# Delta's softplus summed in DRAM by accumulating DMAs, and three W1 products moved up between W2 tiles

## The chip, the cores and the metric

One core of a Trainium2 chip runs the whole program. The metric is the device time of one execution in microseconds (us). The engines are named as the profile names them: PE (TensorE), ACT (ScalarE), DVE (VectorE), POOL (GpSimd) and SP (SyncE, which here only issues DMAs). DMAs issued by SP go through the queue q1, those issued by POOL through q0.

## The reference

x is (4, 2048, 512) in fp32. Two stages follow each other, each with a residual; scale, shift and gate of both come from a conditioning vector c.

```
h = layernorm(x) * (1 + ca) + sa
val, gate = split(h @ W_in);  val = silu(conv3(val))
B, C = val @ W_B, val @ W_C                      # 16 states
Delta = softplus((val @ W_delta + delta_base) @ W_tau)
h_t = exp(Delta*A) * h_(t-1) + expm1(Delta*A)/(Delta*A + 1e-6) * Delta * B_t * val_t   # over 2048 tokens
y_t = sum over the 16 states of h_t * C_t
x = x + ga * ((y * silu(gate)) @ W_out + h)
h = layernorm(x) * (1 + cb) + sb
x = x + gb * (top-2 of 8 experts, gated, plus one shared expert: gelu(h @ W1 + b1) @ W2 + b2)
```

The change touches how Delta's softplus is put together, and the order of some W1 products.

## The kernel before

**Tiling.** The 8192 tokens are cut into 16 quarters (`q`) of 512. The scan works on a unit of 128 channels by 1024 tokens; a unit has 16 states, one **slot** each, so there are 512 slots in a row. A **window** H holds 32 slots, r = 0 to 31. In window H the engines do the scan of slots 32H to 32H+31, and between its steps the attention products of quarter `qa` = H+2 and the expert products of quarter `qf` = H-2; `qn` = H+3 is the quarter that is loaded next. Windows run from -3 to 18; those with both a scan and a quarter `qa` are 0 to 13, and two more quarters are made before the scan begins.

**What sets the order.** Nothing is scheduled by a tool. Each engine runs through the same windows and slots; the functions `sync_slot`, `act_window`, `pe_slot` (by the table in `pe_jobs`), `dve_slot` and `pool_slot` say what each adds in a slot r. An engine's work is in program order, and semaphores hold the engines together.

**A slot's scan work.** ACT makes `inv` (square, Ln, Exp), `th` (Tanh) and `abar` (Exp) in groups of four states, up to some slots ahead. POOL multiplies `inv` by `th` (line 1316, for two slots ahead), multiplies the state by the row of C (line 1295, for the slot before) and issues a DMA that adds the product into `ysum` in SBUF (line 1303); only one of these is in flight, since each waits for the one before. DVE does four passes over PSUM and SBUF (lines 1099, 1106, 1086, 1092) and the scan itself (line 1119). The scan of slot c writes a buffer of three, so it waits until the addition of slot c-3 has landed. PE puts the row of B for the next slot into PSUM (line 1065) as the first thing of its slot; the other products of the slot are queued behind it. At the end of a unit (r = 1 and 17) POOL waits for the last addition and multiplies `ysum` by the gate (line 1309).

**Delta before.** The product with W_tau (kind `p`, slots 9 and 10 on PE) is taken from PSUM by ACT (`take_p`, line 739) into `pre`. ACT makes exp(-|pre|) in `lnw` and, in place, relu(`pre`); DVE rounds `tt1` = (1+e)-1 (`rounded`, line 1147); POOL makes `tt1 - lnw` (`correction`, line 1340); ACT makes Ln(1+e) in `lnw`; POOL subtracts `tt1` (`log1p`, line 1346, slots 16 and 19); DVE adds min(relu, 1e18) and `lnw` (`softplus`, line 1154, at the end of slots 16 and 20); SP stores the half (slots 17 and 21). All this is done in two halves of two channel groups, 128x1024 each. The buffers are borrowed: `pre` is `hT`, `lnw` is `xa` and `tt1` is `uu`. So `xa`'s next contents, the tokens of `qn` (slots 19 and 21 on SP, line 617), can only be loaded when the half is done with, and DVE takes their statistics (`tile_stats`, line 1124) at the end of slots 21 and 22.

**Expert products.** Line 1038 is a W1 product (one hidden half of one expert: 4 matmuls, 8 instructions in the trace), line 1054 a W2 tile (6 matmuls, 12 instructions). Four PSUM banks are passed round the products of all kinds in the order of the table; a product waits until the one before it in its bank has been taken. W1 weights have two buffers.

## Time and profile before

| | us |
|---|---|
| median of 3 runs | 5096.31 (5090.79 to 5102.79) |
| the profiled execution | 5096.16 |
| its span | 5094.4 |
| DVE busy | 4214.9 (83%) |
| ACT busy | 4024.4 (79%) |
| PE busy | 3923.5 (77%) |
| POOL busy | 3723.2 (73%) |

The span is the time from the first instruction to the last; 1.8 us lie around it. Busy times are of the whole span, and the scan runs in only part of it: its first instruction starts at 276.9 us, its last at 4707.1 us. Before it the first two quarters are made, behind it the last expert products. In the 40 slices of the page DVE stands at 9 in nearly every slice of that part. The instructions named in the text are those of window 6 unless it is said otherwise: its slots 9, 16 and 21 end at 2050.77, 2115.12 and 2159.38 us.

### The profile page before, as it was taken

Reading aid. Unit: us, or ns where it says so; the run is one execution under the profiler, and the core shown is the slowest. Engines: PE = TensorE matmul, PEld = TensorE weight load, DVE = VectorE, ACT = ScalarE, POOL = GpSimd, SP = SyncE. Lnnn points to the kernel's source line nnn. Section 1 sums busy time; section 2 is a strip of 40 time slices with the busy share of each in tenths; the row PEclk is TensorE's granted clock in tenths of the full one; section 3 lists DMA queues with packets and bytes.
Section 4 is the critical chain, followed back from the end, with each engine's and each line's share of the span. In section 5 each row is a group of like instructions: output and inputs, shape, how many; then the busy total and the mean of one; then the engine's idle time right before and its main releaser. Section 6 shows DMA issues by size and latency. Waiting matters only on the chain.

```text
span 5094.4 us, 36516 instructions
## 1 busy us (share of the span) xinstructions
PE 3923.5 (77%) x9708; PEld 1628.3 (32%) x9708; DVE 4214.9 (83%) x3766; ACT 4024.4 (79%) x4251; POOL 3723.2 (73%) x2228
## 2 busy tenths in 40 slices
PE   6551232888898888888888888888888876868989
PEld 3210110333333333333333333333333323333443
DVE  1278799999999999999999999999998999999110
ACT  2486788889899898889899888899998988977111
POOL 0188887787888887778888787787788897878101
PEclk8775565899999999999999999898999997979999
DMA  4388876777786877777777878787777777777322
GB/s 136 126 266 244 245 203 196 208 223 225 215 250 193 258 208 227 207 224 220 216 234 219 244 196 251 196 235 207 225 224 213 228 217 196 219 198 216 97 99 75
DMA packets 343640, 1053.92 MB, mean 207 GB/s; under 512 B 40965, under 2 KB 43909, under 8 KB 336134
## 3 DMA queue, kind: packets, MB, share of 16 engines
q1 hardware_dynamic: 274314, 799.91, 45.8%
q0 software_dynamic: 69120, 251.69, 25.8%
q8 instruction: 78, 1.28, 0.1%
q14 instruction: 128, 1.05, 0.1%
HBM read 673.29 MB, written 126.51 MB: 157 GB/s over the span
## 4 chain that ended last, share of the span: by engine, by line
ACT 22%; issue 19%; POOL 17%; PE 17%; DMA 12%; DVE 11%; SPq 0%; POOLq 0%; DVEq 0%; ACTq 0%
DMA ysum<-hs 10%; POOL inv L1316 5%; PE ps L1038 5%; ACT inv L684 4%; POOL hs L1295 4%; PE ps L1054 4%; PE ps L1008 4%; ACT inv L679 3%; DVE ps L1092 2%; DVE ps L1099 2%; ACT th L691 2%; DVE ps L1086 2%; POOL ysum L1303 2%; ACT inv L689 2%; ACT abar L694 2%
## 5 line engine op out<-in xcount | busy, mean ns | idle before, releaser
L1316 POOL TENSOR_TENSOR inv<-inv,th 128x1024 f32<-128x1024 f32 x512 | 1271.8, 2484 | 259.2 <-ACT th L691 256.3
L1295 POOL TENSOR_TENSOR hs<-hs,Cb 128x1024 f32<-128x1024 f32 x480 | 1209.9, 2521 | 63.1 <-DVE hs L1119 42.9
L1038 PE MATMUL ps<-hf,w1r 128*128 128x512 f32 x2304 | 1133.0, 645 | 65.5 <-DMA w1r<-in_W 38.8
L1065 PE MATMUL ps<-Brow,pick 48*128 48x512 bf16 x1024 | 356.9, 433 | 805.9 <-DVE hs L1119 803.0
L1054 PE MATMUL ps<-w2r,hid 128*128 128x512 f32 x1792 | 842.1, 618 | 13.3 <-issue 13.3
L691 ACT ACTIVATE th<-delta,halfA 128x1024 f32<-128x1024 f32 x512 | 583.3, 1139 | 310.6 <-POOL inv L1316 310.5
L1086 DVE TENSOR_TENSOR ps<-ps,us 128x1024 f32<-128x1024 f32 x512 | 628.1, 1227 | 107.3 <-PE ps L1065 106.7
L1303 POOL DMA_DIRECT2D ysum<-hs x480 | 444.5, 926 | 336.9 <-DMA ysum<-hs 324.0
L1099 DVE SCALAR_TENSOR_TENSOR ps<-ps,coef,inv 128x1024 f32<-128x1024 f32 x512 | 658.6, 1286 | 31.9 <-POOL inv L1316 7.4
L1038 PEld LDWEIGHTS ps<-hf,w1r 128*128 128x128 f32 x2304 | 460.9, 207 | 664.4 <-issue 611.6
L1106 DVE SCALAR_TENSOR_TENSOR ps<-nrd,inv_kappa,ps 128x1024 f32<-128x1024 f32 x512 | 659.1, 1287 | 15.0
L1119 DVE TENSOR_TENSOR_SCAN hs<-abar,ps 128x1024 f32<-128x1024 f32 x256 | 583.4, 2279 | 82.8 <-DMA ysum<-hs 82.6
L1092 DVE SCALAR_TENSOR_TENSOR ps<-abar,ps 128x1024 f32<-128x1024 f32 x512 | 617.9, 1207 | 17.6 <-ACT abar L694 17.5
L679 ACT ACTIVATE inv<-nrd,kappa 128x1024 f32<-128x1024 f32 x512 | 551.7, 1139 | 99.5 <-DVE ps L1099 98.5
L1119 DVE TENSOR_TENSOR_SCAN hs<-abar,carry,ps 128x1024 f32<-128x1024 f32 x256 | 598.6, 2338 | 35.6 <-DMA ysum<-hs 35.5
L694 ACT ACTIVATE abar<-delta,negA 128x1024 f32<-128x1024 f32 x512 | 581.6, 1136 | 0.5 <-DVE hs L1119 0.5
L684 ACT ACTIVATE inv<-inv,consts 128x1024 f32<-128x1024 f32 x512 | 547.5, 1137 | 1.5
L689 ACT ACTIVATE inv<-inv 128x1024 f32<-128x1024 f32 x512 | 536.9, 1049 | 1.4
L1054 PEld LDWEIGHTS ps<-w2r,hid 128*128 128x128 f32 x1792 | 342.8, 197 | 485.5 <-issue 482.4
L1065 PEld LDWEIGHTS ps<-Brow,pick 48*128 48x128 bf16 x1024 | 59.0, 97 | 1175.7 <-DVE hs L1119 975.0
L1139 DVE TENSOR_TENSOR x<-ps,x 128x512 f32<-128x512 f32 x256 | 172.5, 682 | 297.5 <-PE ps L1054 268.1
L1333 POOL TENSOR_TENSOR hid<-hid,gbc 128x1024 f32<-128x1024 f32 x96 | 239.5, 2497 | 153.3 <-DMA gbc<-expert_gates 86.7
(157 smaller groups left out, 5237.9 us busy)
## 6 DMA issues: line engine op xcount, KB each, us to landing
Cb<-c_rows SPq DMA_DIRECT2D x512, 512.0 KB, 4.6
ysum<-hs POOLq DMA_DIRECT2D x480, 512.0 KB, 5.4
w2r<-w_scaled SPq DMA_DIRECT2D x144, 512.0 KB, 7.1
w1r<-in_W SPq DMA_DIRECT2D x144, 512.0 KB, 4.7
gbc<-expert_gates SPq DMA_DIRECT2D x128, 256.0 KB, 5.0
aw<-in_W_val SPq DMA_DIRECT2D x64, 256.0 KB, 5.1
xa<-in_x SPq DMA_DIRECT2D x32, 512.0 KB, 6.4
h_residual<-hT SPq DMA_DIRECT2D x16, 1024.0 KB, 7.5
```

The lines of the kernel that those rows point to most:

```text
L679: s.activation(inv[:, c % 6, :], nrd[:, u % 2, :], ACT.Square, bias=1.0, scale=kappa[:, c % N, u % G:u % G + 1]).then_inc(sq_done, 1)
L684: s.activation(inv[:, c % 6, :], inv[:, c % 6, :], ACT.Ln, bias=consts[:, 1:2]).then_inc(ln_done, 1)
L691: s.activation(th[:, c % 2, :], delta[:, u % 2, :], ACT.Tanh, scale=halfA[:, c % N, u % G:u % G + 1]).then_inc(th_done, 1)
L694: s.activation(abar[:, c % 4, :], delta[:, u % 2, :], ACT.Exp, scale=negA[:, c % N, u % G:u % G + 1]).then_inc(abar_done, 1)
L1038: mm = t.matmul(o, w1r[:, n % 2, k, h * P:(h + 1) * P], hf[:, k, :], start=(k == 0), stop=(k == G - 1))
L1054: mm = t.matmul(o, hidden(e)[:, h, tt * P:(tt + 1) * P], w2r[:, e % 3, h, :], start=(grp < 2 and e % 3 == 0 and h == 0), stop=(e % 3 == 2 ...
L1086: v.tensor_tensor(X(c), X(c), us[:, u % 2, :], ALU.mult).then_inc(uB_done, 1)
L1092: v.scalar_tensor_tensor(X(c), abar[:, c % 4, :], 1.0, X(c), ALU.add, ALU.mult).then_inc(p1_done, 1)
L1099: v.scalar_tensor_tensor(X(c), X(c), coef[:, c % N, u % G:u % G + 1], inv[:, c % 6, :], ALU.mult, ALU.mult).then_inc(pw_done, 1)
L1119: v.tensor_tensor_scan(hs[:, c % 3, :], abar[:, c % 4, :], X(c), 0.0 if first else carry[:, u % G, c % N:c % N + 1], ALU.mult, ALU.add).th ...
L1295: gp_.tensor_tensor(hs[:, c % 3, :] if c % N else ysum[:], hs[:, c % 3, :], Cb[:, c % 2, :], ALU.mult).then_inc(hC_done, 1)
L1316: gp_.tensor_tensor(inv[:, c % 6, :], inv[:, c % 6, :], th[:, c % 2, :], ALU.mult).then_inc(thinv_done, 1)
```

## The change

First, Delta. `take_p` moves from ACT to DVE (end of slots 9, 10 and 11) and caps the value there. `log1p` on POOL and `softplus` on DVE are gone. Instead SP stores relu(`pre`) in slots 14 and 15, and POOL issues two DMAs for each half that add into that store in DRAM: the correction `lnw - tt1` (slots 15 and 16) and the logarithm (slots 17 and 20). Each waits for the DMA before it on the same half. The next tokens for `xa` wait for the landing of the logarithm's DMA, and the load of Delta for the next pair of quarters moves on SP from slot 18 to slot 19. Second, in the table of PE, W1 product 12 goes from slot 23 to 22, product 13 from 24 to 23; product 14 stays in 24 and is alone there.

```diff
 def load_unit(u):
-                if g == 0:
-                    sp.wait_ge(st_delta, 64 * k + 48)
-                if g == 2:
-                    sp.wait_ge(st_delta, 64 * (k + 1))
+                if g % 2 == 0:
+                    sp.wait_ge(st_ln[g // 2], 32 * (k + 1))
...
-            if r == 18 and H % 2 and 0 <= (H + 1) // 2 < NK:
-                load_unit(G * ((H + 1) // 2))
...
-            if r in (17, 21) and has(qa):
-                gp = r // 21
-                sp.wait_ge(delta_done, 2 * qa + gp + 1)
-                store_half(delta_d, qa, 2 * gp, 2 * gp + 2, pre[:, 2 * gp:2 * gp + 2, :]).then_inc(st_delta, 16)
+            if r in (14, 15) and has(qa):
+                gp = r - 14
+                sp.wait_ge(a_relu, 2 * qa + gp + 1)
+                store_half(delta_d, qa, 2 * gp, 2 * gp + 2, pre[:, 2 * gp:2 * gp + 2, :]).then_inc(st_delta[gp], 16)
+            if r == 19 and H % 2 and 0 <= (H + 1) // 2 < NK:
+                load_unit(G * ((H + 1) // 2))
             if r in (19, 21) and has(qn):
                 part = r // 21
-                ge(sp, delta_done, 2 * qn - 1 + part)
+                ge(sp, st_ln[part], 16 * qn)
...
-                20: [("w1", qf, 11), ("w2", qf, 0)], 21: [("w2", qf, 1)], 22: [("w2", qf, 2)], 23: [("w2", qf, 3), ("w1", qf, 12)],
-                24: [("w1", qf, 13), ("w1", qf, 14)], 25: [("w1", qf, 15)], 26: [("w1", qf, 16), ("w1", qf, 17)],
+                20: [("w1", qf, 11), ("w2", qf, 0)], 21: [("w2", qf, 1)], 22: [("w2", qf, 2), ("w1", qf, 12)], 23: [("w2", qf, 3), ("w1", qf, 13)],
+                24: [("w1", qf, 14)], 25: [("w1", qf, 15)], 26: [("w1", qf, 16), ("w1", qf, 17)],
...
-            def softplus(q, gp):
-                if has(q):
-                    part = slice(2 * gp, 2 * gp + 2)
-                    dve.wait_ge(a_log1p, 2 * q + gp + 1)
-                    dve.wait_ge(a_relu, 2 * q + gp + 1)
-                    v.scalar_tensor_tensor(pre[:, part, :], pre[:, part, :], DELTA_HI, lnw[:, part, :], ALU.min, ALU.add).then_inc(delta_done, 1)
+            def take_p(q, g):
+                if has(q):
+                    dve.wait_ge(st_h, 16 * (q + 1))
+                    dve.wait_ge(mm_p, G * q + g + 1)
+                    v.tensor_scalar(pre[:, g, :], ps[:, bank_of["p", q, g], :], tau_bias[:, g:g + 1], DELTA_HI, ALU.add,
+                                    ALU.min).then_inc(ev_p, 1)
...
+            def delta_rows(q, gp):
+                return delta_d[q // 2, 2 * gp:2 * gp + 2, :, (q % 2) * T:(q % 2 + 1) * T].rearrange("g p t -> p g t")
+
+            def add_correction(q, gp):
+                if has(q):
+                    pool.wait_ge(a_corr, 2 * q + gp + 1)
+                    pool.wait_ge(st_delta[gp], 16 * (q + 1))
+                    gp_.dma_start(delta_rows(q, gp), tt1[:, 2 * gp:2 * gp + 2, :], accum_op=ALU.add).then_inc(st_corr[gp], 16)
+
+            def add_log(q, gp):
+                if has(q):
                     pool.wait_ge(a_ln, 2 * q + gp + 1)
-                    gp_.tensor_tensor(lnw[:, part, :], lnw[:, part, :], tt1[:, part, :], ALU.subtract).then_inc(a_log1p, 1)
+                    pool.wait_ge(st_corr[gp], 16 * (q + 1))
+                    gp_.dma_start(delta_rows(q, gp), lnw[:, 2 * gp:2 * gp + 2, :], accum_op=ALU.add).then_inc(st_ln[gp], 16)
...
-            if r in (16, 19):
-                log1p(qa, r // 19)
...
             add_to_y(c - 1)
+            if r in (15, 16):
+                add_correction(qa, r - 15)
+            if r == 17:
+                add_log(qa, 0)
+            if r == 20:
+                add_log(qa, 1)
```

What this makes of the order on POOL, from the addition into `ysum` of slot 14 to that of slot 19, in the middle of the program (lines are numbered as in each kernel; before: 1303 addition to `ysum`, 1295 times C, 1346 `log1p`, 1316 weight, 1309 gate of y, 1333 gating of an expert):

```order
L1303 DMA ysum<-hs 128x1024
L1295 TENSOR_TENSOR hs<-hs,Cb 128x1024
L1346 TENSOR_TENSOR xa<-xa,uu 128x1024
L1316 TENSOR_TENSOR inv<-inv,th 128x1024
L1303 DMA ysum<-hs 128x1024
L1309 TENSOR_TENSOR gy<-ysum,gy 128x1024
L1295 TENSOR_TENSOR ysum<-hs,Cb 128x1024
L1316 TENSOR_TENSOR inv<-inv,th 128x1024
L1295 TENSOR_TENSOR hs<-hs,Cb 128x1024
```

```order
L1295 DMA ysum<-hs 128x1024
L1341 DMA delta_rows<-uu 128x2x512
L1287 TENSOR_TENSOR hs<-hs,Cb 128x1024
L1308 TENSOR_TENSOR inv<-inv,th 128x1024
L1295 DMA ysum<-hs 128x1024
L1341 DMA delta_rows<-uu 128x2x512
L1301 TENSOR_TENSOR gy<-ysum,gy 128x1024
L1287 TENSOR_TENSOR ysum<-hs,Cb 128x1024
L1308 TENSOR_TENSOR inv<-inv,th 128x1024
L1347 DMA delta_rows<-xa 128x2x512
L1287 TENSOR_TENSOR hs<-hs,Cb 128x1024
```

The second piece is the changed kernel, where 1295 is the addition to `ysum`, 1287 times C, 1308 the weight, 1301 the gate of y, 1341 `add_correction` and 1347 `add_log`. The subtraction in slot 16 is gone, and three DMAs stand behind the slots' other work; the fourth follows the addition of slot 19 in the same way.

On PE, slots 22 to 26 before (1065 row of B, 1054 W2 tile, 1038 W1 product of 4 matmuls):

```order
L1065 MATMUL ps<-Brow,pick 128x512 x2
L1054 MATMUL ps<-w2r,hid 128x512 x6
L1065 MATMUL ps<-Brow,pick 128x512 x2
L1054 MATMUL ps<-w2r,hid 128x512 x6
L1038 MATMUL ps<-hf,w1r 128x512 x4
L1065 MATMUL ps<-Brow,pick 128x512 x2
L1038 MATMUL ps<-hf,w1r 128x512 x8
L1065 MATMUL ps<-Brow,pick 128x512 x2
L1038 MATMUL ps<-hf,w1r 128x512 x4
L1065 MATMUL ps<-Brow,pick 128x512 x2
L1038 MATMUL ps<-hf,w1r 128x512 x8
```

and in the changed kernel (1054 row of B, 1043 W2 tile, 1027 W1 product):

```order
L1054 MATMUL ps<-Brow,pick 128x512 x2
L1043 MATMUL ps<-w2r,hid 128x512 x6
L1027 MATMUL ps<-hf,w1r 128x512 x4
L1054 MATMUL ps<-Brow,pick 128x512 x2
L1043 MATMUL ps<-w2r,hid 128x512 x6
L1027 MATMUL ps<-hf,w1r 128x512 x4
L1054 MATMUL ps<-Brow,pick 128x512 x2
L1027 MATMUL ps<-hf,w1r 128x512 x4
L1054 MATMUL ps<-Brow,pick 128x512 x2
L1027 MATMUL ps<-hf,w1r 128x512 x4
L1054 MATMUL ps<-Brow,pick 128x512 x2
L1027 MATMUL ps<-hf,w1r 128x512 x8
```

One product has gone from the fourth row of B's slot to the first; the last slot shown is as it was.

## Rows read from the trace of the kernel before

**Rows 1.** The page's first part: busy us, share of the span, instructions.

```profile
PE 3923.5 (77%) x9708; PEld 1628.3 (32%) x9708; DVE 4214.9 (83%) x3766; ACT 4024.4 (79%) x4251; POOL 3723.2 (73%) x2228
```

**Rows 2.** Busy time by stretch: slots 9 to 8; 17 to 21. PE, PEld, DVE, ACT, POOL.

```profile
2043.54:2323.47 279.93, 239.98 (x603) 98.28 (x602) 266.47 (x233) 250.65 (x265) 223.02 (x120) 0.93 0.77 223
...
2115.12:2159.38 44.26, 37.01 (x84) 14.34 (x82) 43.17 (x28) 38.30 (x40) 34.86 (x19) 0.96 0.74 214
```

**Rows 3.** Groups by line: busy us, mean ns of one, idle before.

```profile
L1154 DVE SCALAR_TENSOR_TENSOR hT<-hT,xa 128x1024 f32<-128x1024 f32 x32 | 96.7, 3025 | 22.6 <-POOL xa L1346 22.6
...
L739 ACT ACTIVATE hT<-ps,tau_bias 128x512 f32<-128x512 f32 x64 | 40.4, 675 | 18.3 <-PE ps L994 18.3
```

**Rows 4.** Line 1154 and 1139 alone: ns min/median/max, first and last start.

```profile
L1154 DVE SCALAR_TENSOR_TENSOR hT<-hT,xa x32: 1211/3038/7297, 149.3 to 4103.9; 128x1024 f32<-128x1024 f32 x32
L1139 DVE TENSOR_TENSOR x<-ps,x x256: 667/680/693, 900.8 to 5091.2; 128x512 f32<-128x512 f32 x128
```

**Rows 5.** DVE in order of time: start, us, [idle before].

```profile
2143.30 2.35 DVE L1119 TENSOR_TENSOR_SCAN hs<-abar,carry,ps 128x1024 f32<-128x1024 f32 x1 [0.60 <-DMA ysum<-hs]
...
2146.68 6.79 DVE L1154 SCALAR_TENSOR_TENSOR hT<-hT,xa 128x1024 f32<-128x1024 f32 x1
...
2169.81 1.27 DVE L1124 BATCH_NORM_STATS2 statsA<-xa 128x6 f32<-128x512 f32 x2
```

**Rows 6.** POOL in order of time, slots 16 to 20.

```profile
2114.64 1.46 POOL L1303 DMA_DIRECT2D ysum<-hs  x1
2122.56 2.35 POOL L1309 TENSOR_TENSOR gy<-ysum,gy 128x1024 f32<-128x1024 f32 x1 [6.46 <-DMA ysum<-hs]
...
2139.61 2.61 POOL L1346 TENSOR_TENSOR xa<-xa,uu 128x1024 f32<-128x1024 f32 x1
...
2146.53 1.14 POOL L1303 DMA_DIRECT2D ysum<-hs  x1
...
2149.48 2.90 POOL L1316 TENSOR_TENSOR inv<-inv,th 128x1024 f32<-128x1024 f32 x1
2155.15 0.88 POOL L1303 DMA_DIRECT2D ysum<-hs  x1 [2.77 <-DMA ysum<-hs]
```

**Rows 7.** DMA queue q0 (packets, MB, share); issues by tile (KB, median us to landing).

```profile
q0 software_dynamic: 69120, 251.69, 25.8%
...
ysum<-hs POOLq DMA_DIRECT2D x480, 512.0 KB, 5.4
...
xa<-in_x SPq DMA_DIRECT2D x32, 512.0 KB, 6.4
...
delta_rows<-hT SPq DMA_DIRECT2D x32, 512.0 KB, 5.8
```

**Rows 8.** Waits of DVE over the whole span: us in total, times, longest.

```profile
DVE hs L1119 <- DMA ysum<-hs: 118.1, 72, 3.9
DVE ps L1086 <- PE ps L1065: 106.7, 80, 8.2
DVE uu L1147 <- ACT xa L749: 79.5, 14, 29.3
```

**Rows 9.** SP's queue in order of time: the second half of `xa`.

```profile
2159.30 0.58 SPq L617 DMA_DIRECT2D xa<-in_x  x1
```

**Rows 10.** PE in order of time, slots 26 and 27.

```profile
2195.27 9.82 PE L1038 MATMUL ps<-hf,w1r 128*128 128x512 f32 x16 [1.62 <-DMA w1r<-in_W]
...
2208.94 3.70 PE L1054 MATMUL ps<-w2r,xn 128*128 128x512 f32 x8 [2.28 <-ACT hid L770]
```

**Rows 11.** DVE in order of time, slots 27 and 28.

```profile
2205.67 1.23 DVE L1086 TENSOR_TENSOR ps<-ps,us 128x1024 f32<-128x1024 f32 x1 [1.61 <-PE ps L1065]
...
2214.93 1.23 DVE L1086 TENSOR_TENSOR ps<-ps,us 128x1024 f32<-128x1024 f32 x1 [1.93 <-PE ps L1065]
```

**Rows 12.** The chain that ended last, before the scan: start us, us, what.

```profile
154.58 6.09 DMA xa<-in_x
...
234.06 2.75 DMA delta_rows<-hT
```

More of the change, by code:

```diff
@@ L393, in adaln_mamba_moe @@
         silu_u, silu_g = sem("silu_u"), sem("silu_gate")
-        a_abs, a_exp, a_relu, a_t, a_corr, a_ln, a_log1p, delta_done = (
-            sem("a_abs"), sem("a_exp"), sem("a_relu"), sem("a_rounded"), sem("a_correction"), sem("a_ln"), sem("a_log1p"),
-            sem("delta_done"))
-        st_gate, st_c, st_b, st_h, st_delta, st_u = (
-            sem("gate_stored"), sem("c_stored"), sem("b_stored"), sem("h_stored"), sem("delta_stored"), sem("u_stored"))
+        a_abs, a_exp, a_relu, a_t, a_corr, a_ln = (
+            sem("a_abs"), sem("a_exp"), sem("a_relu"), sem("a_rounded"), sem("a_correction"), sem("a_ln"))
+        st_delta, st_corr = [sem("relu_stored_0"), sem("relu_stored_1")], [sem("correction_added_0"), sem("correction_added_1")]
+        st_ln = [sem("log_added_0"), sem("log_added_1")]
+        st_gate, st_c, st_b, st_h, st_u = (
+            sem("gate_stored"), sem("c_stored"), sem("b_stored"), sem("h_stored"), sem("u_stored"))
         h_ld, gy_ld, wo_ld, b2_ld, g_st = (
@@ L698, in take_t @@
                 if has(q):
-                    ge(act, st_delta, 32 * q)
+                    ge(act, st_delta[0], 16 * q)
+                    ge(act, st_delta[1], 16 * q)
                     for g in gs:
@@ L713, in take_val @@
                     ge(act, st_u, 16 * q)
-                    ge(act, a_log1p, 2 * q)
+                    ge(act, st_corr[0], 16 * q)
+                    ge(act, st_corr[1], 16 * q)
                     for m in ms:
@@ L732, in silu_of_gate @@
                     s.activation(xa[:], xa[:], ACT.Silu).then_inc(silu_g, 1)
-            def take_p(q, gs):
-                if has(q):
-                    act.wait_ge(st_h, 16 * (q + 1))
-                    for g in gs:
-                        act.wait_ge(mm_p, G * q + g + 1)
-                        s.activation(pre[:, g, :], ps[:, bank_of["p", q, g], :], ACT.Identity,
-                                     bias=tau_bias[:, g:g + 1]).then_inc(ev_p, 1)
             def softplus_exp(q, gp):
@@ L811, in at @@
                         silu_of_gate(qa)
-                    if place == 0:
-                        take_p(qa, (0, 1))
-                    if place == 1:
-                        take_p(qa, (2, 3))
                     if place == 2:
@@ L1224, in late @@
             def late():
+                if r in (9, 10):
+                    take_p(qa, r - 9)
+                if r == 11:
+                    take_p(qa, 2)
+                    take_p(qa, 3)
                 if r == 25 and has(qn):
@@ L1255, in late @@
                     v.tensor_copy(gT, ps[0:EX, bank_of["gT", qf, 0], :]).then_inc(ev_gT, 1)
-                if r in (16, 20):
-                    softplus(qa, r // 20)
                 if r in (21, 22, 23, 24):
@@ L1339, in correction @@
                     pool.wait_ge(a_t, 2 * q + gp + 1)
-                    gp_.tensor_tensor(tt1[:, part, :], tt1[:, part, :], lnw[:, part, :], ALU.subtract).then_inc(a_corr, 1)
-            def log1p(q, gp):
+                    gp_.tensor_tensor(tt1[:, part, :], lnw[:, part, :], tt1[:, part, :], ALU.subtract).then_inc(a_corr, 1)
+            def delta_rows(q, gp):
+                return delta_d[q // 2, 2 * gp:2 * gp + 2, :, (q % 2) * T:(q % 2 + 1) * T].rearrange("g p t -> p g t")
+            def add_correction(q, gp):
                 if has(q):
-                    part = slice(2 * gp, 2 * gp + 2)
+                    pool.wait_ge(a_corr, 2 * q + gp + 1)
[3 more added lines that the diff above has]
+                if has(q):
                     pool.wait_ge(a_ln, 2 * q + gp + 1)
-                    gp_.tensor_tensor(lnw[:, part, :], lnw[:, part, :], tt1[:, part, :], ALU.subtract).then_inc(a_log1p, 1)
+                    pool.wait_ge(st_corr[gp], 16 * (q + 1))
+                    gp_.dma_start(delta_rows(q, gp), lnw[:, 2 * gp:2 * gp + 2, :], accum_op=ALU.add).then_inc(st_ln[gp], 16)
             def newton(u, place):
```

## The prediction

> **What bounds the kernel now.** I read the busy times first. DVE is the busiest engine [rows 1], and in the part where the scan runs it is nearly full: over one period of 32 slots it is busy 266.47 of 279.93 us, ACT 250.65, PE 239.98 and POOL 223.02 [rows 2]. So DVE bounds, and a microsecond taken from it is worth a microsecond as far as the others can follow. Next I read what DVE still waits for: additions into `ysum` (118.1 us), PE's row of B (106.7) and ACT's exponential for `rounded` (79.5) [rows 8]. Of the last, two waits of 29.3 us lie before the scan, which leaves 79.5 - 58.6 = 20.9 us, 1.5 in each of the 14 windows that have both a scan and a quarter `qa`. Last I read slots 16 to 21 on DVE and POOL in order of time [rows 5, 6], since both removed steps sit there: POOL is behind DVE in that place, and DVE waits 0.60 us for an addition in slot 20.
>
> **Removed from DVE.** `softplus`, line 1154, is 32 instructions with 96.7 us, 3.025 each [rows 3], but alone it takes 1.21: the spread is 1.211 to 7.297 [rows 4], and the one at 2146.68 ran until 2153.47 (6.79 us) and outlasted POOL's multiplication of 2149.48, which ended at 2152.38 [rows 5, 6]: it stood while POOL worked. Two a window go: 6.05 us per window on average, 8.0 in window 6 (1.21 and 6.79). When that standing goes, DVE may stand at the next thing it needs from POOL instead. That is the main doubt, worked out below.
>
> **Added to DVE.** Four `take_p` per window read PSUM and write SBUF, 128x512. No such instruction is in the trace; the nearest is line 1139, also 128x512 out of PSUM with an SBUF operand besides, 0.680 us with hardly any spread (0.667 to 0.693) [rows 4]. I take 0.68 each, 2.7 us per window. From below it could be half of that, from above 0.75 plus some waiting for POOL. The Trainium skill (SBUF — State Buffer, "Who interferes with whom") says that a DVE instruction with two SBUF inputs is blocked by a GpSimd one that reads SBUF, and one with at most one SBUF input outside the two-port modes is not; the spread of 1154 against that of 1139 agrees. If `take_p` were blocked as 1154 is, it would cost up to 1.8 us more each, and 4 x 14 x 1.8 = 101 us would turn the result round.
>
> ACT loses its four evictions, 0.675 us each [rows 3], 2.7 us per window. It did them ahead of the exponential that DVE waits for, and DVE comes 2.7 us later to that place, so the 1.5 us of that wait go in full. The PSUM banks of products 2 and 3 come free about 2 us later than before, at the end of DVE's slot 11 instead of ACT's place; the transposes behind them are followed by the row of B, which DVE needs some 2.6 us after it has finished the pass behind `take_p`. I cost that at nothing. Slots 9 to 13 together: +2.7 - 1.5 = **+1.2 us** per window.
>
> **Slots 17 to 21.** They take 44.26 us in window 6 [rows 2]. Without 8.0 of line 1154 and the wait of 0.60 they would take 35.7, 7.1 a slot. Can POOL follow? It issues the last addition of the unit at 2114.64, and the gate of y starts when it has landed, at 2122.56 [rows 6]. Without the subtraction before it (2.35, its sister in slot 19 took 2.61) the issue comes near 2112.3 and the landing 5.4 [rows 7] to 7.9 later (the 7.9 is this one's), say 2119; three multiplications and the issue of the logarithm's DMA (about 1 us, as 0.88 to 1.46 of an addition [rows 6]) bring the next slot to 2127, 2.7 earlier than before. In slot 19 the second subtraction goes too: the addition of 2146.53 comes near 2141.6 and that of 2155.15 near 2148.5, both held by the landing before. DVE, unhindered, would want the first of them landed for its scan of slot 21 at about 2149; it lands 5.4 to 8.6 after 2141.6 (8.6 is the step from 2146.53 to the end of the wait at 2155.15). So about 1 us of new waiting, twice. Slots 17 to 21 end near 2152.9 instead of 2159.38: -6.5 in window 6. Its pair of 1154 was 8.0 against the mean of 6.05, so the mean window gains **-4.5 us**. Bounds: all of 6.05 and the 0.6 (-6.6), or only POOL's own gain in this stretch of two subtractions less two issues, about -2.5.
>
> **The new wait.** The second half of `xa` may be loaded when the second logarithm has landed in DRAM. Before, the load was issued at 2159.30 [rows 9], 6.4 us to landing [rows 7], 2165.7, and DVE took the statistics at 2169.81 [rows 5]: 4 us to spare. Afterwards POOL issues the logarithm behind the addition of slot 19, near 2149.5 to 2150.5. It lands 5.4 later if it goes as an addition into SBUF does, 5.8 is what the plain store of the half takes [rows 7]: 2156 to 2157, SP issues the load, and it lands near 2163.2. DVE, 6.5 us earlier, wants it near 2163.3. That is even, but one of the additions above took 8.6 us to land, and with that the wait is over 2 us; so I put **+1.3 us** per window (0 to 4). Behind the waiting statistics stand DVE's passes of slot 23, and so everything.
>
> The other DMAs: relu is stored in slots 14 and 15, where SP waits for W1 products anyway; the two corrections wait for those stores behind slots 15 and 16, and the second one's wait is hidden by the wait for the last addition (6.46 us at 2122.56 [rows 6]). Four issues on POOL take the place of two multiplications of 2.35 to 2.6: even. On the DMA engines 480 additions are 25.8% of 5094 us [rows 7], 2.7 us of all sixteen each; four more per window are 11 us in 280, which lengthens landings a little.
>
> **W1 products.** Product 16 waits 1.62 us for its weights, which can only be loaded when product 13 is done [rows 10]; with 13 one slot earlier that wait goes, and with it DVE's wait of 1.61 in slot 27 [rows 11]. But the W2 tile of slot 27 waits for ACT to take product 16 out of its bank, until 2208.94 [rows 10], at a place that ACT reaches by its own work. The next row of B is queued behind it, so DVE's wait of 1.93 in slot 28 [rows 11] becomes 1.93 + 1.61. Sum 0 (-1.6 to +1: slots 22 and 23 on PE are each full, near 9 us).
>
> **Before the scan.** The chain runs from quarter 0's Delta to the load of quarter 1's tokens (154.58) and from quarter 1's store (234.06) to the first unit [rows 12]. A subtraction, `softplus` and a store (2.35 + 1.2 + 2.75) give way to two DMAs in series of about 1 + 4.5 each, with nothing to hide them: +3 and +2.5, **+5.5 us** once.
>
> **Sum.** 14 x (1.2 - 4.5 + 1.3 + 0) = -28, with +5.5 -22.5 us. Against the profiled execution's 5096.16 (span 5094.4 and 1.8 around it), which is the median of the runs (5096.31) within 0.2: **5073 us**.
>
> **Rivals.** (a) The lock goes and no wait comes: 14 x (2.7 - 1.5 - 6.6) = -76, +5.5: 5026. For it: POOL loses two multiplications just where it is late. Against it: additions are serial, and the one in flight already held POOL 2.77 us [rows 6]. 0.15.
>
> (b) The wait for `xa` is as long as what slots 17 to 21 give: 2 us over my 1.3 make the window's sum zero, and 5096 + 5.5 is 5102. For it: a margin of 4 us is all there was. Against it: in the middle case worked out above the load comes just in time. 0.18.
>
> (c) Slower: adding in DRAM is slow. Place: the correction stands in q0 ahead of the unit's last addition, and the logarithm ahead of `xa`. Nothing in the trace shows an accumulation into DRAM. If it lands 6 us later than one into SBUF, the gate of y starts some 2.5 us later and POOL carries that through to slot 21, and the statistics wait 4 us more: -2.0 + 2.5 + 4 = +4.5 per window, +63, and +20 before the scan: 5180; with 3 us later it is about 5130. It decides from about 1.6 us later than an addition into `ysum`. The Trainium skill (DMA: Bandwidth & Descriptors, "Anatomy of one DMA — SWDGE (gpsimd) path") says that the receipt of a write is heaviest towards HBM, which is this rival; but stores of the half into DRAM land in 5.8 us by the trace, against 5.4. 0.19.
>
> (d) `take_p` is longer than 0.68 or blocked: at 1.4 each +2.9 per window, 5114. 0.03. The rest, 0.45, is the forecast, which holds 5050 to 5090 by itself.
>
> **How the numbers follow.** No change is within 0.2%, about 10 us: 5086 to 5106. Faster takes (a) and the forecast: 0.60. Same takes (b): 0.18. Slower takes (c) and (d): 0.22. The range cuts the ends of (a) and (c): 5028 to 5118.
>
> **What would show it.** Line 1154 gone and four DVE evictions of 0.68; DVE's wait for ACT's exponential near zero; slots 17 to 21 near 39 us; a wait of DVE's statistics for `xa` of some 20 us in all; logarithms and corrections landing in 5 to 8 us; the wait at slot 27 gone and that at slot 28 longer; the first scan near 282 instead of 276.9. I am wrong if the DMAs into DRAM take 8 us and more, or if the statistics wait over 3 us a window.

## The result, and the profile after

| | before | after |
|---|---|---|
| median of 4 runs, us | 5095.95 (5090.79 to 5102.79) | 5129.48 (5124.58 to 5136.72) |
| ratio | | 1.0057, 95% interval 1.0043 to 1.0071 |
| span of the profiled run, us | 5094.4 | 5134.9 |
| first scan ends, us | 279.2 | 288.1 |
| mean window of 32 slots (windows 2 to 14), us | 277.5 | 279.4 |

The change made the kernel 33 us slower; the prediction was 5073 us, 22.5 faster. The sign is wrong and the time lies 11 us above the range. Window and slot lengths are differences between the ends of successive scans; means are over windows 2 to 14 unless it is said otherwise. Of all executions behind the ratios below one, of `log1_early`, took 13052 us and is left out.

The page's first part after [rows 1]:

```profile
PE 3938.7 (77%) x9708; PEld 1644.7 (32%) x9708; DVE 4157.7 (81%) x3798; ACT 3988.3 (78%) x4187; POOL 3717.6 (72%) x2260
```

DVE has 57 us less to do (forecast: 14 x (6.05 - 2.7) = 47), and the kernel is slower: the work went and more than as much waiting came. DVE's waits [rows 8]:

```profile
DVE hs L1108 <- DMA ysum<-hs: 132.3, 76, 5.3
DVE ps L1075 <- PE ps L1054: 124.5, 61, 8.3
DVE statsA L1113 <- DMA xa<-in_x: 85.5, 18, 21.3
...
DVE ps L1088 <- POOL inv L1308: 43.4, 37, 3.8
DVE ps L1081 <- ACT abar L693: 39.4, 14, 15.5
```

The third row stood at 28.2 us in 6 waits. Two things make its 57 us more: waits before the scan, and one in nearly every window. The same wait from 300 to 4800 us alone, where it was 2.3 us and once before:

```profile
DVE statsA L1113 <- DMA xa<-in_x: 31.3, 13, 5.1
```

So the windows have 29 us of it more, some 2 us each, and the rest lies before the scan, whose first step came only 8.9 us later. The wait for POOL's weight (fourth row) stood at 7.4 in all.

The evictions on DVE, and the rounding behind them, lines 1142 and 1136 (ns min/median/max):

```profile
L1142 DVE TENSOR_SCALAR hT<-ps,tau_bias x64: 737/742/752, 125.7 to 4066.1; 128x512 f32<-128x512 f32 x64
```

```profile
L1136 DVE TENSOR_SCALAR uu<-xa x32: 682/695/4945, 139.6 to 4087.1; 128x1024 f32<-128x1024 f32 x32
  PE ps L988: 5.7, 2
```

`take_p` is 9% above the 0.68 of [rows 4] and has no spread: none of the 64 was held up. The wait for ACT's exponential [rows 8] is gone.

Queue and DMAs after [rows 7], over the whole span:

```profile
q0 software_dynamic: 86528, 285.25, 29.6%
...
ysum<-hs POOLq DMA_DIRECT2D x480, 512.0 KB, 5.8
...
xa<-in_x SPq DMA_DIRECT2D x32, 512.0 KB, 6.4
...
delta_rows<-uu POOLq DMA_DIRECT2D x32, 512.0 KB, 8.8
delta_rows<-xa POOLq DMA_DIRECT2D x32, 512.0 KB, 7.6
```

The corrections (`uu`) land 8.8 us after their issue, which is the first of the two signs that the prediction named for being wrong. The second, a wait for `xa` of over 3 us a window, did not come.

Stretches of window 6: slots 15 to 18 before; then the same after, with slots 17 to 21 [rows 2] (PE, PEld, DVE, ACT, POOL, granted clock, DMA share, GB/s):

```profile
2098.11:2130.50 32.39, 32.20 (x76) 13.08 (x76) 31.90 (x41) 28.90 (x30) 25.76 (x14) 0.94 0.57 144
```

```profile
2119.89:2151.36 31.47, 31.41 (x70) 12.73 (x71) 30.88 (x41) 24.89 (x27) 24.49 (x15) 0.89 0.83 201
2136.91:2176.35 39.44, 36.51 (x84) 14.54 (x83) 35.73 (x26) 37.95 (x41) 32.86 (x18) 0.96 0.93 267
```

In this window slots 17 to 21 did give 44.26 - 39.44 = 4.8 us of the forecast 6.5. But it is not like the others: the same stretch has 39.4 to 46.9 us after, its mean fell only from 43.4 to 43.0. Slot 17, behind the first of DVE's removed additions, fell from 9.4 to 7.2 us and slot 21 from 11.4 to 10.0, but slot 19 grew from 7.2 to 8.3 and slot 20 from 8.3 to 10.3. What changed in every window is the DMA share: mean over windows 2 to 13 from 0.58 to 0.78 in slots 15 to 18, and 0.75 to 0.90 in slots 17 to 21.

Window 9 is the other kind (44.3 us before, 46.9 after). POOL in order of time, slots 16 to 21:

```profile
2969.61 1.50 POOL L1341 DMA_DIRECT2D delta_rows<-uu  x1
...
2976.39 0.89 POOL L1295 DMA_DIRECT2D ysum<-hs  x1 [0.32 <-issue]
2978.95 1.21 POOL L1341 DMA_DIRECT2D delta_rows<-uu  x1 [1.67 <-DMA delta_rows<-hT]
2986.12 2.35 POOL L1301 TENSOR_TENSOR gy<-ysum,gy 128x1024 f32<-128x1024 f32 x1 [5.96 <-DMA ysum<-hs]
...
3019.45 0.87 POOL L1295 DMA_DIRECT2D ysum<-hs  x1 [3.86 <-DMA ysum<-hs]
3020.03 1.52 POOL L1347 DMA_DIRECT2D delta_rows<-xa  x1
```

and DVE's waits there:

```profile
2993.39 1.29 DVE L1088 SCALAR_TENSOR_TENSOR ps<-ps,coef,inv 128x1024 f32<-128x1024 f32 x1 [3.54 <-POOL inv L1308]
3001.77 1.29 DVE L1088 SCALAR_TENSOR_TENSOR ps<-ps,coef,inv 128x1024 f32<-128x1024 f32 x1 [1.32 <-POOL inv L1308]
3008.13 2.29 DVE L1108 TENSOR_TENSOR_SCAN hs<-abar,ps 128x1024 f32<-128x1024 f32 x1 [2.61 <-DMA ysum<-hs]
3019.01 2.29 DVE L1108 TENSOR_TENSOR_SCAN hs<-abar,ps 128x1024 f32<-128x1024 f32 x1 [3.62 <-DMA ysum<-hs]
3033.96 1.29 DVE L1113 BATCH_NORM_STATS2 statsA<-xa 128x6 f32<-128x512 f32 x2 [2.21 <-DMA xa<-in_x]
```

The reader is to follow one delay. The unit's last addition is issued at 2976.39 and the gate of y can start at 2986.12, 9.7 us later, against 7.9 in window 6 before [rows 6]. POOL is late with the weight (3.54), then with the additions (2.61, 3.62), and then with the second logarithm (3020.03), for which `xa` waits (2.21). From the end of the last addition's issue to the gate it is 7.7 us on average (windows 1 to 13, at r = 17), 4.5 before; at the unit ends at r = 1, where no correction is in flight, 4.3 and 4.4.

Before the scan the chain, second quarter [rows 12]:

```profile
230.04 2.87 DMA delta_rows<-hT
233.44 0.89 POOL delta_rows L1341
234.80 7.32 DMA delta_rows<-uu
242.63 6.25 DMA delta_rows<-xa
```

Behind slot 24, PE waits longer in slot 27 for ACT to take product 16 (`hid`), and for weights as long as before. Waits of PE:

```profile
PE ps L1043 <- ACT hid L763: 72.2, 11, 8.2
PE ps L1027 <- DMA w1r<-in_W: 39.9, 14, 5.8
```

The first was 25.6 us in 11 waits before, the second 38.8 in 19. DVE's slots 25 to 28 changed from 8.96, 7.44, 8.70 and 9.51 to 8.09, 7.25, 7.48 and 13.33 us: the wait of slot 27 went and that of slot 28 grew, as forecast, but by 1.5 more than went. Slot 30 gave 1.3 of that back (9.59 to 8.31), so that slots 25 to 31 together took 59.4 us before and 59.6 after.

By place, in us of the mean window, after less before (forecast): slots 9 to 13 -0.7 (+1.2), 17 to 21 -0.4 (-4.5), 23 +1.8 (+1.3), 25 to 31 +0.2 (0), all others +1.0 (0). Together that is +1.9, where -2.0 was forecast.

### The profile page after: what moved, and what is told of

Same layout as the page of the kernel before. It is cut to its first block, busy times and chain, and to the rows that moved or that the text cites. A ratio compares the mean times of both kernels' runs of the same rounds, so it can differ in the third digit from the quotient of the medians.

```text
span 5134.9 us, 36625 instructions
## 1 busy us (share of the span) xinstructions
PE 3938.7 (77%) x9708; PEld 1644.7 (32%) x9708; DVE 4157.7 (81%) x3798; ACT 3988.3 (78%) x4187; POOL 3717.6 (72%) x2260
## 4 chain that ended last, share of the span: by engine, by line
PE 20%; issue 19%; DMA 17%; POOL 17%; ACT 13%; DVE 12%; SPq 0%; POOLq 0%; DVEq 0%; ACTq 0%
DMA ysum<-hs 11%; PE ps L1027 5%; PE ps L1043 5%; POOL inv L1308 4%; POOL hs L1287 4%; PE ps L997 4%; ACT inv L683 3%; DVE ps L1075 3%; DVE ps L1081 2%; DVE ps L1088 2%; ACT inv L678 2%; POOL ysum L1295 2%; DMA delta_rows<-xa 2%; PE ps L971 1%; DMA xa<-in_x 1%
## 5 line engine op out<-in xcount | busy, mean ns | idle before, releaser
L1287 POOL TENSOR_TENSOR hs<-hs,Cb 128x1024 f32<-128x1024 f32 x480 | 1225.9, 2554 | 56.3 <-DVE hs L1108 35.7
L1027 PE MATMUL ps<-hf,w1r 128*128 128x512 f32 x2304 | 1147.9, 651 | 81.4 <-DMA w1r<-in_W 39.9
L1088 DVE SCALAR_TENSOR_TENSOR ps<-ps,coef,inv 128x1024 f32<-128x1024 f32 x512 | 658.2, 1286 | 63.2 <-POOL inv L1308 43.4
L1095 DVE SCALAR_TENSOR_TENSOR ps<-nrd,inv_kappa,ps 128x1024 f32<-128x1024 f32 x512 | 659.1, 1287 | 15.0
L1081 DVE SCALAR_TENSOR_TENSOR ps<-abar,ps 128x1024 f32<-128x1024 f32 x512 | 618.1, 1207 | 39.4 <-ACT abar L693 39.4
L678 ACT ACTIVATE inv<-nrd,kappa 128x1024 f32<-128x1024 f32 x512 | 551.1, 1139 | 67.8 <-DVE ps L1088 65.4
```

Of the source, the lines that this page charges most:

```text
L678: s.activation(inv[:, c % 6, :], nrd[:, u % 2, :], ACT.Square, bias=1.0, scale=kappa[:, c % N, u % G:u % G + 1]).then_inc(sq_done, 1)
L1027: mm = t.matmul(o, w1r[:, n % 2, k, h * P:(h + 1) * P], hf[:, k, :], start=(k == 0), stop=(k == G - 1))
L1081: v.scalar_tensor_tensor(X(c), abar[:, c % 4, :], 1.0, X(c), ALU.add, ALU.mult).then_inc(p1_done, 1)
L1088: v.scalar_tensor_tensor(X(c), X(c), coef[:, c % N, u % G:u % G + 1], inv[:, c % 6, :], ALU.mult, ALU.mult).then_inc(pw_done, 1)
L1095: v.scalar_tensor_tensor(X(c), nrd[:, u % 2, :], inv_kappa[:, c % N, u % G:u % G + 1], X(c), ALU.add, ALU.mult).then_inc(bu_done, 1)
L1287: gp_.tensor_tensor(hs[:, c % 3, :] if c % N else ysum[:], hs[:, c % 3, :], Cb[:, c % 2, :], ALU.mult).then_inc(hC_done, 1)
```

## Experiments

Ratios are to the kernel before in the same batch; 0.001 is 5 us. Slot means are of the one profiled execution, which is not always a typical one: that of the changed kernel lay 7 us above the median of its kernel, those of `evict_w1`, `evict_take16` and `one_add_19` 10, 12 and 14 above, those of `corr1_late` and `sbuf_adds` 12 and 14 below. 13 us are 1 us a window, so differences of slots under that are weak evidence where these are compared.

### The parts one by one

`w1_only` is the kernel before with the new table, `delta_only` the changed kernel with the old one:

```diff
-22: [("w2", qf, 2)], 23: [("w2", qf, 3), ("w1", qf, 12)], 24: [("w1", qf, 13), ("w1", qf, 14)],
+22: [("w2", qf, 2), ("w1", qf, 12)], 23: [("w2", qf, 3), ("w1", qf, 13)], 24: [("w1", qf, 14)],
```

> The kernel before with only the move of W1 products 12, 13 (and 14 alone in slot 24). Theory A, the additions in DRAM cost the time: the move is worth nothing, 5091 to 5101 us, and slot 28 stays near 9.5 us. Theory B, the move costs it: slot 28 grows from 9.5 to about 13 us as in the changed kernel while slots 25 to 27 give back some 2.3, +1.5 us in each of 14 windows, so 5112 to 5122 us.

Measured 1.001 (0.9999 to 1.002): hardly told from nothing. Slot 28 grew to 11.1 us, half of theory B's way, but slots 25 to 31 stayed at 59.5. PE's wait for weights did not go: 36.8 us in 19 waits, against 38.8 in 19.

> The changed kernel with PE's table as before, so only Delta's part. Theory A: all of the loss stays, about 5129 us (5123 to 5135), with slot 28 above 12 us, since ACT is later against DVE. Theory B: the W1 move's +1.5 us a window goes, 5105 to 5112 us, slot 28 near 9.5 us.

Measured 1.003 (1.0021 to 1.004). Neither theory: about half of the loss stays, with slot 28 at 11.5 us. The move costs about 5 us alone (within the noise) and 0.0027, 14 us, on top of Delta's part.

`evict_only` is the kernel before with only this, `evict_back` the changed kernel without it:

```diff
-s.activation(pre[:, g, :], ps[:, bank, :], ACT.Identity, bias=tau_bias[:, g:g + 1])
+v.tensor_scalar(pre[:, g, :], ps[:, bank, :], tau_bias[:, g:g + 1], DELTA_HI, ALU.add, ALU.min)
```

> The kernel before with take_p on DVE, Delta otherwise as before (softplus on DVE and both subtractions on POOL stay). If slots 9 to 13 are even, as the changed kernel's trace has them (-0.1 us), 5090 to 5102 us. A rival: DVE is the bound and 2.7 us more a window cost 1.2 to 2.7 net, 5113 to 5134 us.

Measured 0.9973 (0.996 to 0.9987), 14 us faster, and the fastest kernel here that computes the whole result.

> The changed kernel with take_p on ACT as before (and without the cap at 1e18). Theory A, the additions in DRAM are the loss: no better than the changed kernel, 5125 to 5140 us, the wait of the rounding for the exponential back at 1.5 us a window. The rival, DVE's four evictions are what the removed softplus was exchanged for: 2.7 us a window come back, about 5095 us.

Measured 1.01 (1.008 to 1.012), slower than both theories allowed. Moving `take_p` to DVE gains 14 to 22 us, though it adds 3 us a window to the busiest engine. In `evict_only` slots 9 to 13 take 40.6 us against 40.8, and the wait for ACT's exponential falls from 20.9 us to 0.6 behind 300 us. The rest of the gain is spread: 2.3 us before the scan, 0.2 us a window in slots 4 to 8 and 0.8 in 17 to 21. That it comes from ACT, which has 2.7 us less to do a window, is likely and not shown.

`no_softplus` is `evict_only` without DVE's addition, so its result is incomplete; SP's store waits for POOL's subtraction instead:

```diff
-                if r in (16, 20):
-                    softplus(qa, r // 20)
```

> The kernel before with take_p on DVE, and without DVE's addition of relu and logarithm (relu alone is stored; POOL's subtractions and everything else stay): what the addition on DVE costs, with no DMA in its place. Theory 1, the prediction's: it holds DVE 6 us a window, of which some 4.5 to 6 come back: 14 x 5.2 = 73 us, about 5017 us. Theory 2, DVE waits for POOL in slots 19 to 21 instead of in the addition, since POOL is as far behind as before: 1 to 2 us a window, 5062 to 5080 us.

Measured 0.9942 (0.9927 to 0.9957): 16 us below `evict_only`, theory 2. DVE's busy time falls by about 6 us a window, the window by 1.4. Slot 17 falls from 8.8 to 7.2 us and slot 21 from 11.0 to 9.7, and slot 20 grows from 8.4 to 10.3. Its first wait there:

```profile
DVE hs L1108 <- DMA ysum<-hs: 156.6, 84, 5.9
```

That wait is 100.5 us in `evict_only`. Much of what DVE spent standing in its own addition it now spends standing for POOL's additions into `ysum`.

### The DMAs

`no_corr`, the changed kernel:

```diff
-            if r in (15, 16):
-                add_correction(qa, r - 15)
```

> The changed kernel without the two DMAs of the correction per quarter (POOL still computes it; it isn't added). Theory q0, the corrections in the queue make the unit's last addition land late: the gate of y starts 4.5 us after that addition's issue as before, not 7.7, slots 19 to 21 lose about 2 us, slot 23 stays near 10.8; with 2 to 3 us before the scan 5095 to 5105 us. Theory xa, the late second logarithm is all of it: 5122 to 5130 us.

Measured 0.9983 (0.997 to 0.9995), better than either theory: the corrections' DMAs cost 0.0074, 38 us. 13 of them lie before the scan (its first end is at 274.8 instead of 288.1), where the logarithm waits for the correction's landing and nothing hides it. 2.1 us a window lie after it: 1.0 in slots 17 to 21, where the corrections' effect was looked for, and 1.3 in slots 4 to 8, for which no row shows a cause. The gate starts 5.3 us after the last addition's issue; the wait for `xa` stays (slot 23 10.95 us).

`corr1_late`, the changed kernel:

```diff
-            if r in (15, 16):
-                add_correction(qa, r - 15)
+            if r in (15, 17):
+                add_correction(qa, r // 17)
```

> The changed kernel with the second half's correction issued in slot 17, behind the gate of y, instead of in slot 16. If that DMA is what the unit's last addition shares the DMA engines with, the gate starts 4.5 to 5.5 us after the issue of that addition (7.7 in the changed kernel), slots 19 to 21 get 1.5 to 2 us shorter and the time is 5100 to 5115 us; the first logarithm stands behind the correction then and lands some 3 us later, which slot 22 would show. If the first correction (slot 15) is what delays it, the gate stays at 7 us or more and the time at 5125 to 5135 us.

Measured 1.0103 (1.0084 to 1.0121). The gate stays at 7.6 us: it is the first correction, in slot 15, that delays the unit's last addition. That the kernel became slower than 1.0057 I had not expected, and it stays open: slot 20, where the moved DMA and its logarithm are in flight, has 12.5 us (10.3), but slot 21 gives 1.5 back (8.5 after 10.0).

`sbuf_adds` adds into `pre` in SBUF, and SP stores the sum:

```diff
-gp_.dma_start(delta_rows(q, gp), tt1[:, 2 * gp:2 * gp + 2, :], accum_op=ALU.add)
+gp_.dma_start(pre[:, 2 * gp:2 * gp + 2, :], tt1[:, 2 * gp:2 * gp + 2, :], accum_op=ALU.add)
```

> The changed kernel with the four DMAs adding into the half in SBUF, in the same slots, and SP storing the sum in slots 18 and 21. Theory DRAM, adding in DRAM is what is slow (8.8 and 7.6 us to landing, against 5.8 into SBUF): landings of 5 to 6 us, the wait of the statistics for xa halves, gate of y at 5 to 6 us, 5100 to 5112 us. Theory number, four more accumulations in q0 cost the same wherever they go: landings of 7 us and more, 5125 to 5135 us.

Measured 1.0046 (1.0029 to 1.0063), which can't be told from the changed kernel. Landings:

```profile
hT<-uu POOLq DMA_DIRECT2D x32, 512.0 KB, 8.9
hT<-xa POOLq DMA_DIRECT2D x32, 512.0 KB, 7.2
```

In the windows they are as long into SBUF as into DRAM (8.8 and 7.6), and theory number holds for the time. Two things qualify it. The gate starts 6.8 us after the last addition's issue, 7.7 in the changed kernel; here relu is no longer stored in slots 14 and 15. And before the scan, where little else runs, the target does show, by 1.0 and 1.3 us. The same rows up to 300 us, here and in the changed kernel:

```profile
hT<-uu POOLq DMA_DIRECT2D x4, 512.0 KB, 5.7
hT<-xa POOLq DMA_DIRECT2D x4, 512.0 KB, 5.0
```

```profile
delta_rows<-uu POOLq DMA_DIRECT2D x4, 512.0 KB, 6.7
delta_rows<-xa POOLq DMA_DIRECT2D x4, 512.0 KB, 6.3
```

`corr_store`, `no_corr` with plain stores of the corrections on q1:

```diff
+            if r in (16, 17) and has(qa):
+                sp.wait_ge(a_corr, 2 * qa + r - 15)
+                store_half(corr_d, qa, 2 * gp, 2 * gp + 2, tt1[...]).then_inc(st_corr[gp], 16)
```

> The changed kernel without the correction's DMAs on POOL, but with two plain stores of the same halves by SP (q1) into a spare place in DRAM, in slots 16 and 17: the same bytes out of SBUF at the same time, in the other queue and without adding. The sum in DRAM lacks the correction. Theory engines, the 16 DMA engines are full in slots 15 to 18 (share 0.58 without the corrections, 0.83 with them), so any 512 KB more there delay the unit's last addition: gate of y 6.5 us or more after its issue, ratio 1.002 to 1.005. Theory accumulation, it is the adding DMAs in q0 that hold up the addition behind them: gate at 5.3 us as without them, ratio 0.998 to 1.000.

Measured 1.0038 (1.0024 to 1.0052), gate at 6.8 us. Slots 15 to 18 of window 6 in `no_corr`, and in `corr_store`:

```profile
2086.70:2118.17 31.47, 31.41 (x72) 12.79 (x73) 30.88 (x41) 28.82 (x31) 22.25 (x12) 0.91 0.58 151
```

```profile
2111.85:2143.32 31.47, 31.42 (x71) 12.78 (x72) 30.88 (x40) 25.07 (x28) 24.28 (x14) 0.90 0.70 191
```

Plain stores in the other queue bring back 28 of the 38 us, as theory engines said. So most of the loss needs neither q0 nor the adding, and `sbuf_adds` shows that it doesn't need DRAM as the target either; what all three have in common is more bytes on DMA engines that already are busy there. The 10 us that are left are at the edge of the noise, and POOL had a part in the changed kernel that it hasn't here: 1.5 us for each issue, and 35 us of waits for the stores of relu ahead of them.

### The second logarithm and xa

`log1_early`, the changed kernel:

```diff
-            if r == 20:
+            if r == 19:
                 add_log(qa, 1)
```

> The changed kernel with the second half's logarithm added in slot 19 instead of 20. Theory xa: the statistics' wait in slot 23 (1.8 us a window) shrinks to below 0.8 and the time falls by most of it, to a ratio of 1.002 to 1.0035 (5107 to 5115 us). Theory cover: slots 25 to 31 end together with the experts' products whatever slot 23 does (they took 59.5 us within 0.4 in every kernel so far), the wait moves there: ratio 1.005 to 1.007. A DMA more in slot 19, where DVE waits for the additions of slots 17 to 19, can also cost 0.5 us a window.

Measured 1.0021 (1.0009 to 1.0032), 18 us less than the changed kernel. DVE's wait for `xa`:

```profile
DVE statsA L1113 <- DMA xa<-in_x: 63.1, 6, 22.0
```

Of it 8.0 us in two waits lie behind 300 us, instead of 31.3 in 13, and slot 23 is at 8.93 us, as before. Theory xa holds. One slot of POOL's order was worth more than half of the loss, though the kernel still is 11 us behind the one before.

`one_add` lets POOL subtract the correction from the logarithm as before, and adds once per half; `one_add_19` has its second DMA in slot 19 and the old table:

```diff
+            if r in (16, 19):
+                log1p(qa, r // 19)
-            if r in (15, 16):
-                add_correction(qa, r - 15)
```

> The changed kernel's Delta with one DMA per half: POOL subtracts the correction from the logarithm as before (slots 16 and 19), and only the result is added in DRAM (slots 17 and 20); W1 products as in the changed kernel. Against the kernel without DVE's addition (ratio 0.9942) it has these two DMAs and the W1 move. Theory 1, each accumulating DMA takes its place on the DMA engines and costs about what the corrections did (38 us for 28 of them in windows and the prologue): ratio 0.999 to 1.002. Theory 2, only those that meet a unit's last addition cost, these two don't: ratio 0.995 to 0.998.

Measured 1.0032 (1.0021 to 1.0043), above both theories. Less the 0.0027 of the W1 move that is 0.0063, 32 us, above `no_softplus`. The place tells more than the total: 8 us lie before the scan (first end at 279.0 against 270.8) and 1.75 a window in slot 23 (10.78 against 9.03), the wait for `xa`; slots 17 to 21 grew by 0.6 and the gate starts 4.8 us after the issue, almost as before. Slots 4 to 8 grew by 1.8, as they did by 1.1 for the W1 move in `evict_w1` below. So this pair of DMAs seems to cost mainly by what waits for it in series, and not by its load on the engines, which was theory 1.

> One DMA per half (the corrected logarithm), the second in slot 19 instead of 20, and PE's table as before. If the parts add as they did so far (1.0032 with the W1 move and slot 20; the move 0.0025, slot 20 0.0036): ratio 0.996 to 0.998. If DVE then waits for additions in slots 20 and 21, because the DMA stands ahead of that of slot 19: 0.999 to 1.002.

Measured 0.9984 (0.9974 to 0.9994), close to the first forecast. So one form of the sum in DRAM does reach, and by 8 us pass, the kernel before; it has `take_p` on DVE and stays behind `evict_only`, which has no such DMA. Slot 23 is at 8.93 us, and slot 21 took 0.5 more than in `one_add`.

### The W1 move

> The kernel before with take_p on DVE and the move of the W1 products, Delta otherwise as before. If the two simply add (ratio 0.9973 and 1.001): 0.998 to 0.999 of the kernel before. If the move costs more once ACT's order has changed, as the changed kernel against the one with Delta's part alone suggests (+14 us): ratio 1.000 to 1.001, slot 28 above 12.5 us. If it becomes free: 0.996 to 0.998.

`evict_only` with the new table measured 0.9998 (0.9986 to 1.0009): the move costs 13 us where `take_p` is on DVE. But not in the place that was expected: slot 28 is at 11.6 us, not above 12.5 (10.9 in `evict_only`), and slots 25 to 31 take 59.7 in both. `take16_logs` (the changed kernel) and `evict_take16` (`evict_only`) let ACT take products 16 and 17 earlier:

```diff
-                    if place == 0:
+                    if place == "logs":
                         take_w1(qf, 8)
```

> The changed kernel with ACT taking W1 products 16 and 17 from their banks ahead of the exponentials of slot 28's state group (after the logarithms) instead of behind the first group's. In the changed kernel PE's W2 tile of slot 27 stands 6.0 us on average for that taking (2.1 in the kernel before) and then runs at 7.7 instead of 5.9 us. Theory bank: the taking comes some 4.4 us earlier, slot 28 falls from 13.3 to 9.5 to 10.5 us, the tile to below 6.5 us, and the ratio to 0.998 to 1.002 (1.0057 in the changed kernel). Theory floor: slots 25 to 31 take 59.5 us whatever stands in them, since ACT's exponentials come 1.25 us later for it; slot 28 gets shorter and 29 to 31 longer, ratio 1.004 to 1.007.

> The kernel before with take_p on DVE and the same earlier taking of products 16 and 17. Its W2 tile stands 3.1 us and runs 6.7 us. Theory bank: ratio 0.992 to 0.995, slot 28 from 10.9 to below 9.5 us. Theory floor: 0.9965 to 0.999, as without it.

Measured 1.0091 (1.0075 to 1.0106) and 1.0031 (1.002 to 1.0042), 17 and 30 us slower than without it, and above the ranges of both theories. Of theory bank only the direction in slot 28 was right (10.8 and 9.8 us, each 0.3 above what it allowed). In `evict_take16` the tile's stand (PE's wait for ACT ahead of it) fell from 3.2 to 0.2 us, the tile from 6.7 to 5.3, and slot 28 from 10.9 to 9.8. But slot 29 rose from 7.65 to 10.25, since PE now stands one job later:

```profile
2223.82 1.88 PE L1042 MATMUL ps<-w2r,hid 128*128 128x512 f32 x4
2230.54 1.75 PE L964 MATMUL ps<-identity,xa 128*128 128x128 f32 x7 [4.84 <-ACT hT L702]
```

and ACT at that time:

```profile
2227.64 1.15 ACT L691 ACTIVATE th<-delta,halfA 128x1024 f32<-128x1024 f32 x1 [2.36 <-POOL inv L1316]
...
2229.73 1.43 ACT L702 ACTIVATE hT<-ps,modc 128x512 f32<-128x512 f32 x2
```

The transposes wait for ACT's `take_t`, ACT for POOL's weight. Here slots 25 to 31 took 61.6 us instead of 59.7: a job taken earlier on ACT moved the wait on to a worse place.

What the longer stand does to the tile itself shows in window 6. Stand and tile before, then in the changed kernel (columns as above):

```profile
2206.66:2208.94 2.28, 0.00 (x0) 0.00 (x1) 2.28 (x2) 2.28 (x4) 1.52 (x1) 1.00 0.00 0
2208.94:2212.60 3.66, 3.66 (x9) 1.75 (x10) 3.52 (x4) 3.66 (x5) 3.66 (x3) 1.00 0.46 87
```

```profile
2222.66:2227.03 4.37, 0.00 (x1) 0.01 (x1) 3.08 (x3) 4.36 (x6) 1.52 (x1) 0.86 0.02 8
2227.03:2233.50 6.47, 6.47 (x9) 2.86 (x10) 3.21 (x3) 6.47 (x8) 6.47 (x5) 0.57 0.43 81
```

After a stand of 2.28 us the tile's first eight instructions run with the granted clock at 1.00 (2.4 GHz) and take 3.7 us. After 4.37 us, in which the clock already falls (0.86), they run at 0.57, most of it at 1.2 GHz, and take 6.5. Over windows 2 to 13 the whole tile takes 5.9 us before and 7.7 after, its stand 2.1 and 6.0. A wait on PE is paid again in the work behind it, and the next row of B stands behind that. What this brings the window is another matter: slots 25 to 31 together changed by 0.2 us.

## Why the prediction was wrong

The measured loss, split by the chain of kernels (ratios as above, each difference uncertain by about 0.002, 10 us). The third and fourth row assume that the W1 move costs in `no_corr` what it costs on top of `delta_only`, 0.0027; no run shows that:

| step | ratio | us |
|---|---|---|
| `take_p` to DVE | 0.9973 | -14 |
| DVE's addition away | 0.9942 | -16 |
| logarithm's DMAs in, POOL's subtractions out (`no_corr` less 0.0027) | 0.9956 | +7 |
| corrections' DMAs | 1.003 | +38 |
| W1 move | 1.0057 | +14 |

**Slots 17 to 21: -4.5 a window forecast, -0.4 measured.** This is the step that failed: "So about 1 us of new waiting, twice". The 4.1 us by which it missed are 57 us over 14 windows, as much as the whole miss of 5129 against 5073; that the other terms cancel (slots 9 to 13 better by 27 us, the rest worse by about as much) is chance. Two things were wrong in the step. First, 6.05 us a window of line 1154 were not 6.05 us of path: even with no DMA in their place 1.1 to 1.4 us come back (`no_softplus`). DVE stood in the addition while POOL was behind, and what it gains in slot 17 when that addition is gone, it stands for POOL in slot 20. The prediction saw this ("may stand at the next thing it needs from POOL") and priced it from the one window it had opened, 6, which did gain 4.8. Second, the landing of the unit's last addition was left as it was, while the corrections are in flight beside it: the gate starts 7.7 instead of 4.5 us after its issue.

**The DMA engines.** "11 us in 280, which lengthens landings a little" is the mean over a window. The four DMAs all lie in slots 15 to 20, where the mean share was 0.58 to 0.75 and went to 0.78 to 0.90. That term should have been read from those slots. The corrections' DMAs are the largest cost of the table, 38 us, but not all of it is this load: 13 are the series before the scan, about 14 lie in slots 17 to 21, and for the rest, in slots 4 to 8, the cause stays open.

**Rivals.** (a) fell with slots 17 to 21, (b) since `xa` cost 1.8 and not 3.3 us a window, (d) since `take_p` took 0.742 and was never blocked. **Rival (c)** had the right place, the sign, and "the correction stands in q0 ahead of the unit's last addition". Its "with 3 us later it is about 5130" even is the measured time, and the corrections did land 3 us later than an addition into `ysum` (8.8 against 5.8), the logarithms 1.8. That the totals meet is luck: for 6 us later it had the gate late by 2.5 us, where 3.2 were measured at 3, and it took the gain of DVE's addition as given. Its cause was mostly another. The Trainium skill (DMA: Bandwidth & Descriptors, "Anatomy of one DMA — SWDGE (gpsimd) path") makes the write receipt towards HBM the heavy one. Before the scan the traces agree (6.7 and 6.3 us into DRAM, 5.7 and 5.0 into SBUF); in the windows, where the engines are loaded, landings were the same with SBUF as the target (8.9 and 7.2 us against 8.8 and 7.6), so that rule does not carry the loss there. Plain stores cost most of it.

**The wait for `xa`:** +1.3 forecast, +1.8 in slot 23 measured, and 18 us of the whole when it is taken away. Mechanism right, size inside its bounds. **Before the scan:** +5.5 forecast, +8.9 measured; the DMAs in series take 7.3 and 6.3 us with their issue, where 1 + 4.5 was put.

**Slots 9 to 13:** +1.2 forecast, -0.7 measured there (-0.2 in `evict_only`), and `evict_only` is 14 us faster in all. `take_p` at 0.742 instead of 0.68 was the smaller error. The larger was to ask only what DVE pays in those slots and not what ACT's 2.7 us may give elsewhere.

**W1 products:** 0 forecast, 14 us measured. The time did move from slot 27 to 28 as said, but not for the reason given: the wait for the weights of product 16 did not go (`w1_only`: 36.8 us against 38.8). Slots 25 to 31 together kept their length where the move was made alone or with `take_p` on DVE (59.4 to 59.5, 59.7 to 59.7); on top of Delta's part they grew by 0.8, where the longer stand and the lower clock of the tile may have a share. So why the move costs 5 us alone and 13 with `take_p` on DVE stays open: in `evict_w1` 1.1 of the 1.5 us a window lie in slots 4 to 8, for which I have no row that explains them, and its profiled execution was 10 us above its median.

## What to carry to other kernels

Work taken from the busiest engine is worth only what the engines behind it let it use: before counting it, look at what that engine needs some slots later, in several windows and not in one. Price a DMA by the share of the DMA engines in the slots where it flies and not by their mean, and by what waits for its landing; in the loaded slots here neither its queue nor its target mattered much. Where one engine's load is moved to the bound one, both sides count: here the bound engine got 3 us a window more and the kernel got faster.
